# Attention values as stationary weights in four column groups, and ready-made sums of H's parts before the last LSTM states

## The reference, cut to what matters

```
h = relu(layernorm(x))                       # layer 0: masked attention, 4 heads of 32
q, k, v = split(h @ W)                       # per batch, per head
attn = softmax(q @ k.T / sqrt(32) + mask)    # 128 x 128 per batch and head
x = x + attn @ v
h = relu(layernorm(x))                       # layer 1
h = relu(adj @ (h @ Wg0 + bg0))
h = relu(adj @ (h @ Wg1 + bg1))              # H, 64 x 128 x 128
for p in 1..4:                               # an LSTM over every window of p tokens
    h[:, last token of each window] = last LSTM state of the window
x = x + h
```

## Time and profile before

| what | value |
|---|---|
| median of 3 runs | 554.71 us |
| profiled execution, device time | 551.66 us |
| profiled execution, span | 549.9 us |
| mean granted TensorE clock | 0.973 |
| TensorE matmul busy | 503.4 us (92%) |
| VectorE busy | 427.7 us (78%) |
| ScalarE busy | 352.6 us (64%) |
| GpSimd busy | 170.3 us (31%) |

### The profile page before, as it was taken

One profiled execution on the slowest core, in us unless ns is written; L12 is line 12 of the kernel. 1 busy time (PEld: TensorE's weight loads), 2 busy tenths in 40 slices (PEclk: granted clock), 3 DMA queues, 4 the chain that ended last, 5 costly groups with the idle time before them and its releaser, 6 DMA issues.

```text
span 549.9 us, 10009 instructions
## 1 busy us (share of the span) xinstructions
PE 503.4 (92%) x3464; PEld 434.2 (79%) x3464; DVE 427.7 (78%) x918; ACT 352.6 (64%) x573; POOL 170.3 (31%) x179
## 2 busy tenths in 40 slices
PE   3788999999999999999979999999999999999653
PEld 3577888888888888888867778889999888888533
DVE  3866787778877788776783788888888888788896
ACT  2445866668666686767757777777766577656241
POOL 2434424454344543541110012111121212233473
PEclk9999999999999999999998999999999999999975
DMA  7323000000000000000000000000000000000134
GB/s 216 102 81 92 2 2 1 2 0 0 0 0 0 0 0 0 0 0 1 2 1 0 2 0 1 1 0 2 1 1 1 2 0 1 0 1 20 58 95 134
DMA packets 18778, 11.29 MB, mean 21 GB/s; under 512 B 662, under 2 KB 17724, under 8 KB 18748
## 3 DMA queue, kind: packets, MB, share of 16 engines
q1 hardware_dynamic: 17052, 10.03, 6.3%
q10 hardware_dynamic: 1696, 0.87, 0.6%
HBM read 6.70 MB, written 4.19 MB: 20 GB/s over the span
## 4 chain that ended last, share of the span: by engine, by line
PE 62%; DVE 20%; ACT 8%; issue 6%; DMA 2%; POOL 1%; DVEq 0%; ACTq 0%; SPq 0%; POOLq 0%
PE ps L900 19%; PE ps L838 10%; PE ps L747 7%; PE ps L758 6%; DVE arena L1220 4%; DVE S_hi L1214 3%; PE ps L851 3%; DVE arena L1201 3%; PE ps L779 3%; PE ps L795 3%; PE ps L856 2%; ACT arena L587 2%; PE ps L942 2%; DVE arena L1191 2%; PE ps L769 2%
## 5 line engine op out<-in xcount | busy, mean ns | idle before, releaser
L601 ACT ACTIVATE arena<-ps,bias 128x512 f32<-128x512 f32 (+1 forms) x207 | 120.8, 626 | 38.3 <-PE ps L900 36.8
L565 ACT ACTIVATE arena<-ps 128x512 f32<-128x512 f32 (+1 forms) x112 | 85.5, 790 | 50.0 <-PE ps L758 42.3
L545 POOL TENSOR_TENSOR arena<-arena 128x512 f32<-128x512 f32 (+1 forms) x36 | 44.1, 1225 | 168.1 <-ACT arena L601 168.1
L900 PE MATMUL ps<-H_hi,W_hi 128*128 128x512 f32 (+2 forms) x207 | 76.0, 367 | 6.5 <-DVE S_lo L1216 5.1
L900 PE MATMUL ps<-H_lo,W_hi 128*128 128x512 f32 (+2 forms) x207 | 75.2, 363 | 0.0
L900 PE MATMUL ps<-H_hi,W_lo 128*128 128x512 f32 (+2 forms) x207 | 75.0, 362 | 0.0
L838 PEld LDWEIGHTS ps<-arena 128*128 128x128 f32 x512 | 64.1, 191 | 12.6 <-issue 8.4
L747 PE MATMUL ps<-ident,arena 128*128 128x128 f32 x384 | 54.6, 291 | 17.7 <-DVE arena L1220 7.8
L504 POOL TENSOR_TENSOR veps<-mv,eps 128x4 f32<-128x4 f32 x32 | 11.7, 365 | 187.0 <-DVE mv L1070 187.0
L838 PE MATMUL ps<-arena 128*128 128x33 f32 x512 | 63.5, 269 | 3.5 <-ACT arena L565 2.1
L747 PEld LDWEIGHTS ps<-ident,arena 128*128 128x128 f32 x384 | 46.1, 150 | 21.1 <-issue 9.3
(11 more groups left out here) (106 smaller groups left out, 1021.0 us busy)
## 6 DMA issues: line engine op xcount, KB each, us to landing
X<-in_x_dram SPq DMA_DIRECT2D x16, 256.0 KB, 2.8
out_dram<-X SPq DMA_DIRECT2D x14, 256.0 KB, 2.3
out_dram<-X ACTq DMA_DIRECT2D x2, 256.0 KB, 3.1
arena<-in_L_gnn_W_dram ACTq DMA_DIRECT2D x1, 128.0 KB, 3.0
wg<-in_L_gnn_Wg_dram ACTq DMA_DIRECT2D x2, 64.0 KB, 2.3
bg_rows<-in_L_gnn_bg_dram SPq DMA_DIRECT2D x6, 0.5 KB
wv<-in_L_gnn_W_dram ACTq DMA_DIRECT2D x1, 64.0 KB, 3.2
adj_sb<-in_adj_dram SPq DMA_DIRECT2D x1, 64.0 KB, 3.3
```

The source lines that it names most:

```text
L545: g_.tensor_tensor(ig[:, it.buf, 0:w], sig_i[:, it.buf, 0:w], tanh_g[:, it.buf, 0:w], ALU.mult)\
L565: a_.activation(to, psum, func).then_inc(ready, 1)
L601: a_.activation(to[:, it.buf, 0:w], ps[:, 4 * it.par + j, 0:w], func, bias=bias[:, col:col + 1])\
L900: l = mm(o, wt, v, start=m == 0, stop=m == len(terms) - 1)
```

## The change

Stage 1: the values become the stationary weights, 32 columns per head, and the probabilities stream past them; head h writes PSUM partitions 32h to 32h+31. The sums of the exponentials come from four products with a block of ones, spread over the same 32 partitions. The result is the transposed attention output, so VectorE takes the reciprocal of a whole bank, multiplies, TensorE transposes back (`attended`), and VectorE adds to `X` in the next turn from PSUM (`add_attention`). `read_v` no longer leaves room for ones. On TensorE k's projection moves behind the first mix and the second transposes behind the first graph product; on ScalarE the relu of `hn2` and the read of `u1T` move ahead; on VectorE `normalize` of layer 1 moves ahead of the second `shift`.

Stage 2: `add_parts` fills `h_sums` (two chunks deep) in H's own order before the last states exist, at places listed in `PARTS`; `final_state` replaces `state`, `split` and `whole` for every chunk of p = 4 and writes the last tokens in. The OUT item's transposes read `h_sums` with a stride. ScalarE evicts nothing there, GpSimd adds nothing to `X`; VectorE adds all 16 groups from PSUM (`add_output`). OUT0 and OUT1 stand right behind (1,3) and (2,3). ScalarE's gates are counted in `steps` instead of `n`, and an item that takes over the banks of an OUT item waits on TensorE for `out_ready`.

```diff
+                    if p == MAX_SKIP and CHUNKS[p] <= d < last_diagonal and d - t == CHUNKS[p] - 1:
+                        straight(p, OUT, d - CHUNKS[p])
...
-            if p == MAX_SKIP and CHUNKS[p] <= d < last_diagonal:
-                straight(p, OUT, d - CHUNKS[p])
...
-        return it.n * 4 + (j + 1 if it in early else j - 3)
+        return it.steps * 4 + (j + 1 if it in early else j - 3 + 4 * it.follows)
...
+        psO, psSum = ps[:, 4, :], ps[:, 5, :]
...
     def iteration(s):                                # ScalarE
                 if s.mid:
                     read_probT(s, 0)
+                read(hn2, hn2, xn2_ready, k - 1, hn2_ready, ACT.Relu)
                 if s.next1:
                     read_hT(psX[s.back], k + 2, 1 - s.par)
+                read(u1T[:], psA, u1_done, k - 1, u1T_ready)
                 if s.finish:
...
-                read(hn2, hn2, xn2_ready, k - 1, hn2_ready, ACT.Relu)
...
-                read(u1T[:], psA, u1_done, k - 1, u1T_ready)
...
-            def attend(s, half):
-                def part(b):
-                    if b == 0:
-                        pe.wait_ge(probT_ready, s.k * 2 - 1 + half)
-                    for h in (2 * half, 2 * half + 1):
-                        o = b * 2 + h % 2
-                        l = mm(psO[:, half, o * (HD + 1):(o + 1) * (HD + 1)], probT[:, h, b * N:(b + 1) * N],
-                               v_sb[:, 1 - s.par, b, h, :], start=True, stop=True)
...
+            def attend(s):
+                pe.wait_ge(probT_ready, s.k * 2)
+                for h in range(HEADS):
+                    l = mm(psSum[h * HD:(h + 1) * HD, :], ones_f[:, 0:HD], probT[:, h, :], start=True, stop=True)
+                l.then_inc(att_sums, 1)
+                for b in range(GB):
+                    at_ = slice(b * N, (b + 1) * N)
+                    for h in range(HEADS):
+                        l = mm(psO[h * HD:(h + 1) * HD, at_], v_sb[:, 1 - s.par, b, h, :], probT[:, h, at_],
+                               start=True, stop=True)
+                l.then_inc(att_done, 1)
+
+            def attended(s):
+                pe.wait_ge(att_read, s.k)
+                transposed(psSum, batches(att)).then_inc(attT_done, 1)
...
+                if it.reuse:
+                    pe.wait_ge(out_ready, it.reuse)
                 if it.t == OUT:
                     for j in range(OUT_GROUPS):
                         pe.wait_ge(gate_acts, banks_free(it, j))
-                        pe.wait_ge(h_sum, it.chunk * OUT_GROUPS + (j + 1))
...
+                        pe.wait_ge(h_sum, 2 * it.chunk + 1 + j // HALF)
+                        transposed(ps[:, 4 * it.par + j, :], by_token_batch_first(h_sums[:, it.chunk % 2, j, :]))\
                             .then_inc(gate_sums, 1)
...
     def iteration(s):                                # TensorE, behind first_gate(s, 0, 0)
-                if s.mid:
-                    if s.front:
-                        pe.wait_ge(q_ready, k + 1)
-                    interleave([], attend(s, 0))
...
                 interleave([], graph_mix(hn2, u1_done))
-                if s.mid:
-                    transpose_prob(s, 1)
+                if s.front:
+                    if s.next1:
+                        pe.wait_ge(hT_hi_ready, k + 2)
+                    pe.wait_ge(x2_ready, k - 1)
+                    interleave([], project(s, psK, D, k_done))
                 pe.wait_ge(u1T_ready, k - 1)
...
                 graph_linear_1().then_inc(z1_done, 1)
+                if s.mid:
+                    transpose_prob(s, 1)
                 first_gate(s, 1, 2)
...
-                interleave(attend(s, 1), masks)
+                attend(s)
                 if s.front:
                     scores()
+                attended(s)
                 pe.wait_ge(h1_ready, k - 1)
                 interleave([], graph_mix(h1, u2_done))
...
+            def over_sums(s):
+                dve.wait_ge(att_sums, s.k)
+                v_.reciprocal(rec, psSum).then_inc(rec_ready, 1)
+                dve.wait_ge(rec_ready, s.k)
+                dve.wait_ge(att_done, s.k)
+                if not s.prep:
+                    dve.wait_ge(attT_done, s.k - 1)
+                v_.tensor_tensor(att, psO, rec, ALU.mult).then_inc(att_read, 1)
+
+            def add_attention(k):
+                dve.wait_ge(attT_done, k - 1)
+                xg = X[:, ds(k * GB - 2 * GB, GB), :]
+                v_.tensor_tensor(xg, xg, psSum.rearrange("p (b d) -> p b d", b=GB), ALU.add).then_inc(x2_ready, 1)
+                dve.wait_ge(x2_ready, k - 1)
+                moments(1, k - 2, stats2, var2)
...
+            def add_parts(chunk, groups):
+                p = MAX_SKIP
+                dve.wait_ge(steps, done_at[p - 1, p - 2, 2 * chunk + 1])
+                for j in groups:
+                    at_ = slice((chunk * OUT_GROUPS + j) * GT, (chunk * OUT_GROUPS + j + 1) * GT)
+                    v_.tensor_tensor(h_sums[:, chunk % 2, j, :], H_hi[:, at_].bitcast(F32), H_lo[:, at_].bitcast(F32),
+                                     ALU.add).then_inc(parts_added, 1)
+            PARTS = {(0, 0): (0, (0, 1)), (1, 0): (0, (2, 3)), (0, 1): (1, (0, 1)), (1, 1): (1, (2, 3)),
+                     (2, 2): (2, (0, 1)), (3, 1): (2, (2, 3)), (3, 2): (3, (0, 1, 2, 3))}
+            def final_state(it):
...
+                for m in range(2):
+                    part = slice(m * HALF, (m + 1) * HALF)
+                    v_.tensor_tensor(to[:, part], o[:, part], c[:, part], ALU.mult).then_inc(h_sum, 1)
...
+            def add_output(it, js):
+                for j in js:
+                    g = it.chunk * OUT_GROUPS + j
+                    dve.wait_ge(gate_sums, it.n * 4 + (j + 1))
+                    xg = X[:, g * GB:(g + 1) * GB, :]
+                    v_.tensor_tensor(xg, xg, batches(ps[:, 4 * it.par + j, :]), ALU.add).then_inc(out_ready, 1)
```

More of the change, by code:

```diff
@@ L69, in gnn_block, with __init__ @@
     class Item:
-        def __init__(self, p, t, chunk, n, par, buf, slots, later, steps, needs, ahead, waits):
+        def __init__(self, p, t, chunk, n, par, buf, slots, later, steps, splits, needs, ahead, waits):
+            self.splits = splits
+            self.follows, self.reuse = 0, 0
             self.needs, self.ahead = needs, ahead
@@ L132, in gnn_block @@
                     assert all(it.needs + r * it.ahead >= rounds[r][m].needs for r in range(LOOPED[p]))
-                    assert all(it.needs + r * it.ahead < rounds[r][m].steps for r in range(LOOPED[p]))
+                    assert all(it.needs + r * it.ahead < rounds[r][m].splits for r in range(LOOPED[p]))
                 segments.append((LOOPED[p], rounds[0]))
@@ L531, in visit @@
             def visit(it, prev):
[L532 to L540 removed]
+                if it and it.t != 0 and it.t != OUT:
                     w = width(it.p)
@@ L609, in visit @@
                     return
-                outputs = range(OUT_GROUPS) if it and it.chunk < CHUNKS[MAX_SKIP] - 1 else range(0)
-                for j in outputs:
-                    if prev.t != OUT and j == (OUT_GROUPS - 1 if is_last(prev) else 0):
-                        tanh(prev)
-                    act.wait_ge(gate_sums, it.n * 4 + (j + 1))
-                    a_.activation(h_out[:, j, :], ps[:, 4 * it.par + j, :], ACT.Copy).then_inc(gate_acts, 1)
+                if prev.t != OUT:
+                    tanh(prev)
             def read_hT(psum, count, par):
@@ L982, in fill @@
                     pe.wait_ge(k_ready, k + 1)
-                    interleave(attend(s, 1), [lambda h=h: put_mask((h,)) for h in (2, 3)])
+                    put_mask((2, 3))
+                    attend(s)
                 else:
@@ L1238, in whole @@
[L1238 to L1247 removed]
+                dve.wait_ge(parts_added, (it.chunk + 1) * OUT_GROUPS)
@@ L1249, in visit @@
             def visit(it, prev):
-                if prev and prev.t != OUT and is_last(prev):
-                    last_state(prev)
-                    return
+                out = it and it.t == OUT
+                first = HALF if out and it.chunk == CHUNKS[MAX_SKIP] - 2 else 0
+                if first:
+                    add_output(it, range(first))
                 if prev and prev.t != OUT:
-                    state(prev)
-                    if not (it and it.t == 0):
-                        split(prev)
@@ L1258, in visit @@
[L1258 to L1272 removed]
+                    if is_final(prev):
+                        final_state(prev)
+                    else:
+                        state(prev)
+                        if not (it and it.t == 0):
+                            split(prev)
@@ L1274, in last_iteration @@
+                if it and not out:
+                    cell_part(it)
+                if prev and prev.t != OUT and it and it.t == 0 and not is_final(prev):
+                    split(prev)
+                if it and it.p == MAX_SKIP and (it.t, it.chunk) in PARTS:
```

(3 more changed lines are left out.)

182 lines of the change are left out of this document (61 added, 121 removed).

## The result

The changed kernel takes 587.37 us in the median (586.70 to 590.29, 4 runs) beside 555.57 us for the kernel before in the same comparison: a ratio of 1.060, 95% interval 1.053 to 1.066. (A ratio is taken over all the runs; that of these two medians is 1.057.) It is slower by 31.8 us; forecast was 582 against 554.71, slower by 27.3. The kernel before has executions from 550.3 to 552.2 us and others from 554.7 to 556.7, and three of its four here are of the second kind, so the profiled execution of 551.66 and the later medians of 551.2 to 551.9 put the loss at 35.5 to 36 us.

What follows compares the result with a forecast made beforehand. TensorE was taken to bound steady stage 1 and VectorE the last 50 us. 551.66 + 44 (stage 1) + 1.4 - 18.6 (stage 2) = 578.5 us, plus 3.05 to the median, rounded 582; range 545 to 612.

Steps and rivals of the forecast that it cites:

- TensorE's own work: Stage 1: attend's 3.56 us removed, sums and values 1.10 each and transposes 0.4 added, about 0.9 us less a turn.
- rival E: Stage 1: column groups do not overlap, sums 3.4 and values 3.5 us, turn 22.5, +78, 616 us; chance 0.08.
- The reciprocal: Stage 1, VectorE: 512 elements instead of 8, at 7.1 ns each on 0.15 us fixed, 3.8 us.
- rival B: Stage 1: the reciprocal runs nearly like a copy, 0.68 to 1.7 us, total 542 to 550 us; chance 0.18.
- The new waits: Stage 1, TensorE: 2.6 us for VectorE ahead of att's transposes, 0.7 us for hn2 ahead of the first mix, each turn.
- R: Time of the 512-element reciprocal on VectorE in stage 1, taken as 3.8 us within a turn of 16.40 us plus it.
- Rival D: Stage 1: the clock falls in the turns, 1.3 us a turn in 14 turns, +18, 600 us; chance 0.15.
- The turns: Stage 1: a turn of 20.2 us, 2.9 more than before, over 15 turns: +44 us.
- Stage 2: The tail: VectorE ends 18.6 us earlier, +1.4 us once where p = 4 begins; 17.2 us gained.
- wait at `reuse`: Stage 2's end: only 12 us gained if adds and sums collide with TensorE's reuse waits once per item.
- The +1.4 us at the start of p = 4: Stage 2: two sums of 0.71 us on VectorE ahead of the split TensorE waits for, +1.4 us once.
- The sum: Whole kernel: 551.66 + 44 + 1.4 - 18.6 = 578.5 us as profiled, 582 for the median.

Runs made afterwards that it cites:

- experiment 4: The changed kernel with eight unused products of 512 columns on TensorE between scores and the transposes of att: 574.45 us, ratio 1.039.
- experiment 3: The changed kernel with a copy of the sums in place of the 128x512 reciprocal, so no division: 539.74 us, ratio 0.977.
- experiment 7: The kernel before with only the new stage 2, sums of H's parts made just ahead of a chunk's last products: 541.04 us, ratio 0.984.
- experiment 5: The changed kernel with the transposes of att moved behind the second mix and the third first gate on TensorE: 581.18 us, ratio 1.055.
- experiment 10: The changed kernel with the division moved behind the transposes, four small products bringing the sums to 16 elements a partition: 571.62 us, ratio 1.033.
- experiment 8: The kernel before with only the new stage 2, plus 14 unused GpSimd additions beside the sums of H's parts: 541.77 us, ratio 0.982.
- experiment 9: The kernel before with only the new stage 2, sums of H's parts written at a stride as before: 541.94 us, ratio 0.978.

## Why the prediction was right, and where it was off

**TensorE's own work.** Right in kind, even too dear: the sums took 0.88 and the values 0.99 us for the 1.10 taken from `scores`, the transposes 0.5 for 0.4. Column groups overlap; rival E is out.

**The reciprocal.** Taken as 3.8 us, measured 3.35, so rival B (up to 1.7 us) is out. The estimate came from the median of the earlier trace rows over the copy's fixed part; the shortest of the same row would have given 1.7, so that the choice of the median, on one size, carried the forecast. The slope it gave was 7.1 ns, measured 5.4 to 6.4 by pairs of sizes. The repeat count of 8 in the Trainium skill ("VectorE: DVE Perf Modes", section "First, the fixed hardware budget"), read as 8 cycles an element, gave an estimated 4.4 us. With this reading the trace disagrees: 6.4 ns are about 6 cycles at the page's 0.96 GHz.

**The new waits.** 2.6 us forecast ahead of the transposes, 2.3 measured; 0.7 for `hn2`, 0.5 measured. Forecast turn 16.40 + R = 20.2 us; with the measured R it would be 19.75, and with the clock up it was 19.4 to 19.5.

**The clock.** Rival D (0.15) came true beside the forecast, not in its place. The prediction's chances treated the two as alternatives; the filled wait shows that both hold at once, and prices the clock at 12.9 us, for the 18 given. Without it the kernel would have met the forecast from below, 574.5 for 582. "TensorE: Matmul & The Clock Gate" of the Trainium skill, section "HAM oscillation — how this bites in real kernels", wants longer idle stretches than these before the clock falls; by that the trace disagrees, with granted clocks of 0.91 in stretches whose longest gap is 2.4 us.

**The turns.** 15 turns at 2.9 were to give +44. From the first `scores` to the last the 15 turns took 302.1 us (18.70 to 320.84) for 257.3 (19.17 to 276.47): +44.8, or 20.1 a turn for the 20.2 forecast. That the two agree is luck: the reciprocal was taken too dear by 0.45 us a turn and the waits by 0.3, and the low clock, which the forecast left out, filled the place. With the clock up the 13 turns from the third `scores` on take 252.5 us (experiment 4), in the changed kernel 264.0.

**The ends of stage 1.** Left out. From the last `scores` to stage 2's first product it is 28.8 us for 20.9, +7.9, where the forecast has nothing. With the copy of experiment 3 it is 21.5, with the filled wait 26.2, so about 4.7 us are the reciprocal's and 2.7 the clock's. The last group shows why: no `scores` stands beside the reciprocal, so 3.85 us of wait in place of 2.3. With 0.5 us less ahead of the first `scores`, stage 1 is at 52.3 for 44.

**Stage 2.** -17.2 forecast, -16.6 measured. By its pieces: VectorE's last add to `X` ends 231.3 us after the first product for 248.9 before, -17.6, and the last stores took 1.0 us more behind it. No wait at `reuse` showed. The +1.4 us at the start of p = 4 came, as 1.26. VectorE, then TensorE; the kernel before has no wait of TensorE between 440 and 510 us:

```profile
495.06 1.29 DVE L1230 TENSOR_TENSOR arena<-H_hi,H_lo 128x512 f32<-128x512 f32 x2
```

```profile
498.91 0.49 PE L901 MATMUL ps<-H_hi,W_hi 128*128 128x512 f32 x1 [1.26 <-DVE S_lo L1221]
```

In experiment 7, where no sums stand there, this wait is gone. The size was luck: the prediction read two sums in 1.42 us from a piece of a chain, but the shortest of the old sums took 1.03 us; 0.69 is the price in the new order. Most of what the end gained is TensorE's waits there, 7.8 us for the sums, 3.0 for ScalarE's evictions and this one:

```profile
520.16 0.74 PE L900 MATMUL ps<-H_hi,W_hi 128*128 128x512 f32 x1 [4.12 <-DVE S_lo L1216]
```

**The sum.** 44 + 1.4 - 18.6 = +26.8 us forecast, 52.3 - 16.6 = +35.7 by the spans, 31.8 by the medians. So by the profiled executions the forecast was 8.9 us short, and nearly all of it is the ends of stage 1. The 582 lies only 5.4 us under 587.37 because 3.05 us were added for the median of the kernel before, while the changed kernel's median equals its profiled execution.

## What to carry to other kernels

Before an operation is moved to another layout, count its elements per partition: the matmul side gained a microsecond, and the reciprocal went from 8 elements to 512 in the one place where TensorE had nothing else to do. A wait inside a ring of engines isn't removed by moving it down the queue (experiment 5). Try the halves of a combined change alone: one half here was worth 15 us and was buried under the other's 53. And compare stretches of the traces beside the medians: in experiments 7 to 9 the medians were off by up to 2.7 us through a stage that no edit touched.

## What the runs showed that I had not expected

- **Filling an idle wait made the kernel faster.** 8 useless products a turn took 12.9 us off, as the granted clock stayed at 1.00 instead of falling to 0.91.
- **A product with 4 columns costs no less than one with 128.** In experiment 10 the eight instructions of `128x4` take 0.99 us from their start (175.28) to that of `scores` (176.27), the eight of `128x128` of the mix 0.82 (177.86 to 178.68).
- **VectorE at half speed beside GpSimd.** 0.69 to 1.41 us for the same instruction of two inputs (experiment 8). The Trainium skill, "SBUF — State Buffer", section "🔬 SBUF: two separate sides", tells of a pair of ports that the two take in turn as an exclusive lock; the rows agree with that in size, and do not tell it from a shared rate.
- **A strided write costs VectorE 0.4 us in 128x512**: 1.12 in the median for 0.69 (experiment 9).
